# Query-row energies ahead of the transposed energies in each half step of an attention kernel

## The reference, cut to what matters

```python
scores = jnp.einsum('bhqd,bhkd->bhqk', Q, K) / np.float32(np.sqrt(DK))
if mask is not None:
    scores = jnp.where(mask[:, None, :, :] == 0, jnp.float32(-1e+20), scores)
A = jax.nn.softmax(scores, axis=-1)
out = jnp.einsum('bhqk,bhkd->bhqd', A, V).transpose(0, 2, 1, 3).reshape(b, sq, D)
```

## Time and profile before

| | us |
|---|---|
| median of three executions | 2907.93 (2906.82 to 2912.08) |
| the profiled execution | 2903.91 |
| its span, first to last instruction | 2902.1 |
| TensorE matmuls busy | 2543.9 (88%) |
| TensorE weight loads busy | 1408.3 (49%) |
| VectorE busy | 1797.3 (62%) |
| ScalarE busy | 1407.6 (49%) |
| GpSimd busy | 753.1 (26%) |

### The profile page before, as it was taken

The page is one execution under the profiler, slowest core; times in us unless marked ns, Lnnn a source line. Parts: engine busy times, 40 slices in busy tenths (PEclk is TensorE's granted clock), DMA queues, the critical chain, the costliest instruction groups (busy, mean ns, idle before and its releaser), DMA issues. The chain is left out here.

```text
span 2902.1 us, 44468 instructions
## 1 busy us (share of the span) xinstructions
PE 2543.9 (88%) x16062; PEld 1408.3 (49%) x16062; DVE 1797.3 (62%) x4375; ACT 1407.6 (49%) x1935; POOL 753.1 (26%) x893
## 2 busy tenths in 40 slices
PE   5998988864799999998899997699999999685886
PEld 2444433323344444443789997234444344473543
DVE  2566777745577777774556774477777777343454
ACT  1444455541255555565347884155555555431333
POOL 3233333326211111110115664112222221123022
PEclk7999999987799999999799998699999999897999
DMA  5112222101232322320117775332322321001431
GB/s 168 47 47 67 54 68 61 47 1 15 76 89 68 104 68 71 90 69 11 59 59 210 219 219 134 79 78 68 109 66 63 92 64 43 1 1 28 101 82 47
DMA packets 103345, 220.82 MB, mean 76 GB/s; under 512 B 19144, under 2 KB 35400, under 8 KB 101848
## 3 DMA queue, kind: packets, MB, share of 16 engines
q1 hardware_dynamic: 94296, 205.92, 26.1%
q0 software_dynamic: 8832, 12.06, 2.3%
HBM read 100.34 MB, written 12.58 MB: 39 GB/s over the span
## 5 line engine op out<-in xcount | busy, mean ns | idle before, releaser
L979 ACT ACTIVATE probT_a<-scores 128x1024 f32<-128x1024 f32 (+3 forms) x832 | 785.2, 950 | 692.1 <-PE scores L832 428.4
L1069 DVE CUSTOM_DVE_ANT_0 ring<-ring,maskb_a 128x512 f32<-128x512 f32 x1024 | 681.1, 720 | 191.7 <-PE ring L850 153.4
L850 PE MATMUL ring<-stacks_a 64*128 64x512 f32 (+7 forms) x1664 | 472.5, 416 | 78.4 <-DMA stacks_a<-fixed_a 22.7
L871 PE MATMUL outputs<-probT_a,V_a 128*32 128x512 f32 (+6 forms) x3328 | 446.6, 580 | 27.1 <-ACT probT_a L979 15.7
L1067 DVE TENSOR_REDUCE negm_a<-ring 128x1 f32<-128x512 f32 (+3 forms) x640 | 329.9, 563 | 163.8 <-PE ring L856 119.4
L811 PE MATMUL scores<-stacks_a 64*128 64x512 f32 (+7 forms) x1664 | 412.1, 476 | 0.0
L811 PEld LDWEIGHTS scores<-stacks_a 64*128 64x128 f32 (+1 forms) x1664 | 164.5, 186 | 428.5 <-issue 321.2
L850 PEld LDWEIGHTS ring<-stacks_a 64*128 64x128 f32 (+1 forms) x1664 | 239.2, 193 | 208.0 <-DVE negm_a L1069 80.8
L1113 DVE SCALAR_TENSOR_TENSOR parts_a<-ring,wcol,parts_a 128x512 fp32r<-128x512 f32 x112 | 84.1, 751 | 243.4 <-ACT parts_a L1017 243.4
L776 POOL TENSOR_SCALAR maskb_a<-maski_a 128x1024 bf16<-128x1024 int32 x32 | 116.5, 3640 | 453.5 <-DMA maski_a<-in_mask 423.9
L832 PE MATMUL scores<-maskT_a,identb 64*64 64x512 bf16 x1024 | 211.0, 402 | 0.0
(11 more groups left out here) (214 smaller groups left out, 3778.0 us busy)
## 6 DMA issues: line engine op xcount, KB each, us to landing
stacks_a<-parts_a SPq DMA_DIRECT2D x672, 128.0 KB
raw<-in_moew SPq DMA_DIRECT2D x92, 512.0 KB, 3.9
maski_a<-in_mask SPq DMA_DIRECT2D x32, 512.0 KB, 3.4
maskS_a<-maskT_a SPq DMA_DIRECT2D x32, 256.0 KB, 3.5
wt<-in_w SPq DMA_DIRECT2D x7, 1024.0 KB, 4.8
kvT_a<-in_ctxT SPq DMA_DIRECT2D x12, 512.0 KB, 3.3
stacks_a<-fixed_a SPq DMA_DIRECT2D x4, 1024.0 KB
wrow<-in_row SPq DMA_DIRECT2D x7, 512.0 KB, 6.1
```

The source lines that it names most:

```text
L850: last = pe.matmul(bank("S", j, n, e)[:, 0:w], Q[rows, g, qt * P:(qt + 1) * P], K[rows, g, 0:w], start=True, stop=not a.causal)
L871: last = pe.matmul(OB[x * slot:(x + 1) * slot, q0:S], V[:, m % 2, kb, c:c + slot], probT[:, kb % 2, x, q0:S], start=(kb == 0), stop=(kb == ...
L979: act.activation(probT[:, kb % 2, 2 * p:2 * p + 2, q0:S], scores_bank(j, n)[:, :, q0:S], ACT.Exp, bias=0.0, scale=-1.0).then_inc(c_exp.sem, 1)
L1069: least = dve.tensor_tensor_reduce(sc, sc, maskb[:, m % 2, qt, :], 1.0, BIG * 2, ALU.add, ALU.min, out)
```

## The change

In `schedule`, S is yielded ahead of ST. SyncE, ScalarE, VectorE and GpSimd take no part in ST, so their orders stay, and so do the ring's turns; TensorE's order changes in every half step that has both.

```diff
         for h in range(halves):
-            if there(j):
-                yield ("ST", j, h)
             if there(j + 2):
                 yield ("S", j + 2, h)
             if there(j):
+                yield ("ST", j, h)
                 yield ("exp", j, h)
```

## The result

The changed kernel takes 2924.64 us (median of 13 runs, 2914.82 to 2931.12) against 2907.93 us for the kernel before: ratio 1.0057, 95% interval 1.0045 to 1.007, so 13 to 20 us slower. The forecast was 2927 us. Its profiled execution has a span of 2920.5 us (before 2902.1), at a granted clock of 0.925 (0.929).

A forecast was written before the change was run, and what follows sets the result against it. TensorE's queue was taken to set the pace; 16 us in the first stage plus 3 in the last, on the profiled 2903.9 us, gave 2923, or 2927 us as a median; 8-in-10 range 2906 to 2946.

The forecast's parts named there:

- What bounds the kernel: Wherever attention runs, TensorE's queue sets the pace; what counts is the distance between starts of its matmul groups.
- The price of the switches: First stage: alternating 64- and 128-row shapes costs 0.30 us per half step, 33.6 us over 112 half steps.
- The 0.09 for leaving the 64-row shape: First stage, ST to CP: leaving the 64-row shape costs 0.09 us more per half step than staying in it.
- its rule on row groups: Weight loads overlap running matmuls only where row groups differ; first stage would cost 0.19 us per half step, 21 us.
- What hides part of it: First stage: S's waits for VectorE absorb 12.6 us, and 4.5 more at batch changes, leaving 16 of 33.6 us.
- The sign named for it: First stage of the changed trace: waits of S for VectorE should fall well under 12.4 us.
- Masked and unmasked stages at 0: Four masked stages and the unmasked one (L0 cross): no change; 10 us either way in the masked stages.
- I take 0: Unmasked stage: exp starts 0.22 us later, but 0.20 of 0.42 us to spare remain, so no loss.
- The loss of up to 21 us by a later exp: Unmasked stage: if the cover were gone in all 64 products, 64 x 0.33 = 21 us would be lost.
- Last stage: Heads fill 128 rows, so only weight loads count: 0 to 11 us over 56 half steps, taken as 3 us.
- Hidden altogether: First-stage switches fall into TensorE's existing waits, last-stage load hides behind P: 2908 us, give or take 6; chance 0.17.
- Slower by more: Nothing hidden in the first stage, full switches in the last, later exp delaying products: 2953 to 2974 us; chance 0.10.

The follow-up runs named there:

- the kernels with the short minimum: VectorE's row minimum of S over 64 columns only in a0, a1 and a6: in the kernel before 2844.03 us, in the changed kernel 2879.73 us.
- the run of a0 alone: Kernel before with S ahead of ST only where ST's tile is in a0: 2926.66 us, ratio 1.0068.
- first in a1 beside ring work: Kernel before with S ahead of ST only in a1's half steps beside projections, transposes or minimum rows: 2904.77 us, ratio 1.0004.
- the mixture: Kernel before with S ahead of ST throughout a2 to a5, in a1 only in half steps without ring work beside them: 2901.36 us, ratio 0.9986.

## Why the prediction was right, point by point

- **What bounds the kernel: right.** The loss shows in the distances between TensorE's groups; the other engines are busy about as long as before.
- **The price of the switches: right.** 0.31 us in an ordinary half step for 0.30; P to ST 0.22 and ST to CP 0.37, the two figures that were to be seen; S's load exposed. The 0.09 for leaving the 64-row shape had been read at a step to 64x64, not to CP's 128x128; at CP it is the same (0.37 for 0.28). That the kernels with the short minimum lie 36 us apart, near the 34 + 3 that were worked out, is luck in part: a0 gives 27.7 of it. By the drain of the Trainium skill alone ("TensorE: Matmul & The Clock Gate", Part 2, step 4), an estimate of 12 us for a0 or 0.11 a half step, the cost would have been a third of what the prediction took; by its rule on row groups (Part 3, The mechanism), 21 or 0.19. Neither agrees with the measured 0.31.
- **What hides part of it: the size is near, the parts differ.** 16 us were to be left; at about equal clock 18 to 20 are, and the run of a0 alone gives 20 (14 to 25). Where they lie can be summed from start to start over a0's timelines, the changed kernel (0.93) against the one with S first in a1 to a5 (0.94), whose a0 has the order of before and is 20 us shorter. P to ST and ST to CP hold 21 us more than ST to S and P to CP held, as 112 x (0.10 + 0.09) has it. S to P is 3.7 us longer, where 112 x 0.11 = 12.3 of exposed load were priced, so S's waits hide over 8. CP to the ring work behind it is 4.3 us shorter; the other distances nearly cancel. So 13 to 14 us are hidden where 17 were forecast, most of it where the prediction had it, and a third in waits of the ring work that no term had. The sign named for it failed: S's waits were to fall "well under 12.4 us", and from 76 to 341 us of the changed kernel the view of waits has:

```profile
PEld ring L849 <- DVE negm_a L1066: 13.0, 27, 1.2
```

  That view counts idle time of the weight loads, in which matmuls may still run (0.84 us of it stands before the load at 193.61, behind a product), so it does not measure what TensorE loses.
  In ordinary tiles they shrink (S of 384 columns at 184.68 waited and reached P after 0.56 before; after, at 194.74, it takes 0.37). One of the other waits stands before a projection, in three of a0's four batches, 1.5 us in all. In one half step of a0, with TensorE's and VectorE's timelines, the kernel before:

```profile
178.18 1.21 DVE L1087 TENSOR_REDUCE amax_a<-X 128x4 f32<-128x1024 f32 x1
...
179.55 0.48 DVE L1067 TENSOR_REDUCE negm_a<-ring 128x1 f32<-128x128 f32 x2
```

```profile
178.41 0.60 PE L895 MATMUL ring<-identf,mx_a 128*32 128x128 f32 x4
179.89 1.99 PE L934 MATMUL ring<-wt,xT_a 128*128 128x256 f32 x8 [0.88 <-DVE negm_a L1067]
```

  and the changed one:

```profile
187.87 1.21 DVE L1086 TENSOR_REDUCE amax_a<-X 128x4 f32<-128x1024 f32 x1
...
189.24 0.48 DVE L1066 TENSOR_REDUCE negm_a<-ring 128x1 f32<-128x128 f32 x2
```

```profile
188.60 0.60 PE L894 MATMUL ring<-identf,mx_a 128*32 128x128 f32 x4
189.57 1.99 PE L933 MATMUL ring<-wt,xT_a 128*128 128x256 f32 x8 [0.37 <-DVE negm_a L1066]
```

  The projection waits for a ring bank that VectorE frees with the first of its two minima, and VectorE is late by its own work (1.21 us of amax), whatever TensorE does. TensorE arrived 0.5 us later, and the wait is 0.51 shorter. No term of the sum had this wait.
- **The clock: not foreseen.** a0's granted clock fell from 0.96 to 0.93 in both profiled executions that have the changed a0 and the full minimum, and 5 to 7 us go with it there. Over the whole kernel the mean clocks of the timed runs differ little (0.926, before 0.928), so this bears on the profile more than on the median. What lowers it was not tried.
- **Masked and unmasked stages at 0: wrong by a few us, in a1 above all.** They gain 0.28% (0.12 to 0.44), about 8 us. In the profile of the change a1 is 4.3 us shorter at its clock of before; the masked stages are 4.1 shorter together, and about 2 of that go with a4's clock (0.99 for 0.98). The step that failed is the one for a1, "I take 0", which weighed only that exp comes later. The prediction's argument that "VectorE gets a bank back exactly as early against its next use" holds in the pair looked at (S waits 0.32 us in either order), but not its conclusion that nothing can be gained: with S first, ST runs beside the S matmul that waited, and the pair takes 1.93 us for 2.10 (last section). This is read from one pair and was not tested by itself. The loss of up to 21 us by a later exp is not seen with the full minimum; between the two kernels with the short one a1 is 2.8 us longer, and whether that is exp was not tested.
- **Last stage: near, in part by luck.** 3 us forecast, 3.2 measured, but at a clock of 0.97 for 0.98. Two experiments that leave a6 as it was (first in a1 beside ring work, and the mixture) had it at 0.97 too, with 175.3 and 175.2 us; against these the change costs 1.2. With the short minimum, at 0.97 in both kernels, it costs 3.7. S of 256 columns reaches P in 0.35 us, where the earlier trace rows have 0.25, and P to ST takes 0.09 for the 0.12 of P to CP in the earlier trace rows:

```profile
2742.87 0.50 PE L849 MATMUL ring<-stacks_a 128*128 128x256 f32 x2
2743.22 0.28 PE L855 MATMUL ring<-causal,identb 128*128 128x128 bf16 x2
2743.31 0.60 PE L810 MATMUL scores<-stacks_a 128*128 128x384 f32 x2
```

- **The rivals.** "Hidden altogether" fails by a0. "Faster, by ST's wait for exp" fails there too: with the shapes kept together (S, ST, P, CP) ST still comes later against exp, and a0 gains nothing. "Slower by more" lies above the 13 to 20 us measured; with VectorE's long minimum out of the way the order cost 36 us in all.

So 2927 met 2925 in part by luck, with errors on both sides: about 4 to 9 us too little in a0, 8 us too much in a1 to a5.

## What to carry to other kernels

Before two groups of matmuls change places, write down the sequence of array shapes: each added change into and out of a 64-row shape was 0.3 us per half step here, and a permutation that kept the shapes together (S, ST, P, CP) cost nothing in that half step. To find what hides such a cost, look at every wait for the late engine behind the moved group, the projections' too, not only at the moved group's own. And when an engine returns buffers late, try the other work between two uses of them, alternating from half step to half step if need be: the kernel so made was 0.48% faster than before, though not clear of S first throughout a1 to a5 (0.28%).

## What was not expected of the hardware

In this kernel 3 to 5 us of a0's 270 go with 0.02 of mean granted clock (rows above), as much as some of the effects that were sought; stages are compared at equal clock, or not at all. And two matmuls on different row halves start together even across S and ST: where S's second matmul has waited, ST's first one (rows 0 to 63, by `place`) starts with it. In a1 of the kernel before, S's second matmul and the ring work behind it:

```profile
475.37 0.49 PE L850 MATMUL ring<-stacks_a 64*128 64x512 f32 x1 [0.32 <-DVE negm_a L1067]
475.97 1.99 PE L934 MATMUL ring<-wt,kvT_a 128*128 128x256 f32 x8
```

The same with S first in a1 to a5 (S L853, ST L814):

```profile
475.26 0.49 PE L853 MATMUL ring<-stacks_a 64*128 64x512 f32 x1 [0.32 <-DVE negm_a L1070]
475.27 0.72 PE L814 MATMUL scores<-stacks_a 64*128 64x512 f32 x2
475.92 0.48 PE L937 MATMUL ring<-wt,kvT_a 128*128 128x256 f32 x1
```

From S's second matmul to the ring work it is 0.60 us before and 0.66 here, with the whole ST in between.
